# Inversion products of two batches packed on four tiles, and their copies made wide

## The reference

```python
# per batch, value head (32) and chunk (8 chunks of 64 tokens)
decay = jnp.where(tril, jnp.exp(g[..., :, None] - g[..., None, :]), 0.0)
M = jnp.where(stril, jnp.einsum('bhncd,bhnmd->bhncm', k_beta, k) * decay, 0.0)
T = jax.scipy.linalg.solve_triangular(eye + M, eye, lower=True)      # 64 x 64
v_c = T @ v_beta;  k_cumdecay = T @ (k_beta * exp(g))
# then a scan over the 8 chunks:
#   v_new = v_i - kcd_i @ state;  out = (q*exp(g)) @ state + (q k^T * dec) @ v_new
#   state = state * exp(g_last) + (k * exp(g_last - g))^T @ v_new
```

## Time and profile before

| | |
|---|---|
| median of 3 runs | 3193.22 us (3192.94 to 3195.3) |
| the profiled execution | 3193.03 us, span 3191.2 us |
| TensorE busy | 2911.1 us (91%) |
| VectorE busy | 1643.1 us (51%) |
| ScalarE busy | 1305.7 us (41%) |
| GpSimd busy | 1782.0 us (56%) |
| mean granted TensorE clock | 0.988 |

### The profile page before, as it was taken

One profiled execution on the slowest core, in us unless ns is written; L12 is line 12 of the kernel. 1 busy time (PEld: TensorE's weight loads), 2 busy tenths in 40 slices (PEclk: granted clock), 3 DMA queues, 4 the chain that ended last, 5 costly groups with the idle time before them and its releaser, 6 DMA issues.

```text
span 3191.2 us, 101541 instructions
## 1 busy us (share of the span) xinstructions
PE 2911.1 (91%) x41680; PEld 2122.0 (66%) x41680; DVE 1643.1 (51%) x2807; ACT 1305.7 (41%) x3046; POOL 1782.0 (56%) x1829
## 2 busy tenths in 40 slices
PE   2899999999999999999999999999999999999889
PEld 1566766766667666667766667677666667766744
DVE  4555555555555555655555555555545655555412
ACT  2443444444444444444444444444444444444311
POOL 1565555656655565665555566655555665555500
PEclk7899999999999999999999999999999999999999
DMA  2111110110111001011110101111011111110020
GB/s 83 27 30 29 30 22 19 27 35 24 30 29 27 20 22 34 24 30 29 30 29 9 35 24 30 30 29 31 13 29 27 29 29 29 30 25 9 3 61 20
DMA packets 71088, 89.52 MB, mean 28 GB/s; under 512 B 16720, under 2 KB 39376, under 8 KB 70608
## 3 DMA queue, kind: packets, MB, share of 16 engines
q1 hardware_dynamic: 70608, 82.74, 10.1%
HBM read 77.64 MB, written 5.08 MB: 26 GB/s over the span
## 4 chain that ended last, share of the span: by engine, by line
issue 35%; POOL 32%; PE 19%; DVE 7%; ACT 2%; POOLq 1%; DVEq 0%; DMA 0%; SPq 0%
POOL hT L1071 10%; POOL hT L1077 5%; PE ps L422 4%; POOL Kd L1094 4%; PE ps_state L537 3%; DVE St L931 3%; PE ps L510 3%; POOL Dm L1012 2%; POOL Sd L1035 2%; POOL Dm L1009 2%; PE ps L557 2%; POOL Kg L1094 2%; PE ps L611 2%; POOL A L1101 1%; PE ps_two L601 1%
## 5 line engine op out<-in xcount | busy, mean ns | idle before, releaser
L1035 POOL TENSOR_TENSOR Sd<-St,el 128x512 f32<-128x512 f32 x192 | 201.3, 1048 | 897.2 <-DVE St L928 843.4
L411 PEld LDWEIGHTS ps<-XW,U 64*64 64x64 f32 x10240 | 317.9, 135 | 125.8 <-issue 123.8
L411 PEld LDWEIGHTS ps<-XW,P 64*64 64x64 f32 x10240 | 311.8, 135 | 119.8 <-issue 119.8
L1071 POOL TENSOR_SCALAR hT<-idx_s,lutb 128x134 f32<-128x134 int32 x480 | 355.4, 744 | 27.5
L411 PE MATMUL ps<-XW,U 64*64 64x64 f32 x10240 | 342.9, 220 | 17.2 <-issue 12.7
L411 PE MATMUL ps<-XW,P 64*64 64x64 f32 x10240 | 333.6, 220 | 0.0
L834 DVE SCALAR_TENSOR_TENSOR cacc<-ps_two,cw,cacc 128x1022 f32<-128x1022 f32 (+2 forms) x192 | 245.7, 1280 | 97.1 <-ACT cacc L638 92.5
L923 DVE TENSOR_TENSOR Vn<-ps,bR 128x256 f32<-128x256 f32 x256 | 108.6, 424 | 350.3 <-PE ps L484 296.7
L834 DVE SCALAR_TENSOR_TENSOR cacc<-ps_state,cw,cacc 128x1022 f32<-128x1022 f32 (+2 forms) x192 | 245.7, 1280 | 78.5 <-ACT cacc L638 73.9
L382 PE MATMUL ps_two<-xnT,w_qkv 128*128 128x512 f32 x512 | 261.8, 636 | 20.4 <-DVEq L838 18.5
L711 ACT ACTIVATE P<-ps 128x512 f32<-128x512 f32 x320 | 184.2, 595 | 229.9 <-PE ps L411 229.3
(11 more groups left out here) (140 smaller groups left out, 5552.7 us busy)
## 6 DMA issues: line engine op xcount, KB each, us to landing
qg<-g_scratch SPq DMA_DIRECT2D x64, 512.0 KB, 7.4
g_st<-g_scratch SPq DMA_DIRECT2D x64, 256.0 KB, 5.7
w_qkv<-in_wqkvz SPq DMA_DIRECT2D x16, 512.0 KB, 3.8
w_z<-in_wqkvz SPq DMA_DIRECT2D x16, 256.0 KB, 3.1
w_o<-in_wout SPq DMA_DIRECT2D x16, 256.0 KB, 3.3
idx_s<-in_idx SPq DMA_DIRECT2D x32, 67.0 KB, 1.8
fw_scratch<-looked_up SPq DMA_DIRECT2D x32, 67.0 KB, 1.9
Kg<-in_x SPq DMA_DIRECT2D x2, 1024.0 KB, 7.6
```

The source lines that it names most:

```text
L411: m = pe.matmul(bank[r, c * C:(c + 1) * C], left[r, b, c, :], right[r, b, c, :], start=True, stop=True)
L1035: pool.tensor_tensor(Sd[:, :, :, :], St[:, c % 2, :, :, :], el[:, R.par, :, :, c].unsqueeze(3).broadcast_to([P, BB, RATIO, P]), ALU.mult). ...
L1071: m = pool.tensor_scalar(slots[k], idx_s[:, :], float(k), lutb[:, k:k + 1], ALU.is_equal, ALU.mult)
```

## The change

Both batches go through each step of the inverse together. `products` issues, for each chunk and head, one matmul of batch 0 on a diagonal tile and one of batch 1 on a tile off the diagonal, so that the four 64 x 64 tiles of the array are used in turn. A first product of batch 1 writes its result on the other half of the partitions; the second product therefore reads X of batch 1 from a copy with the halves exchanged, `Xs`, which ScalarE makes with two instructions per level (`swap`). The P1 copy, the masked copy and the turn become one instruction each for both batches, with masks twice as long in the constants. The banks 2 to 5 hold the two results (`ps_p1`, `ps_p2`); the four uses of `begin` go over four banks, no longer three; the last turn of the output moves from bank 5 to bank 1. VectorE issues the taps of kind lv - 2 at the end of level lv, one level later than before, and ScalarE its silu of a kind one level later too (the last one after the z gates).

```diff
-    small = [("z", i) for i in range(4)] + (N2 if nxt else []) + [("out", i) for i in range(4)]
+    small = [("z", i) for i in range(4)] + (N2 if nxt else [])
...
-        wide += [("p1", (lv, b)) for b in range(BB)] + [("p2", (lv, b)) for b in range(BB)]
+        levels += spread([("p1", (lv, b)) for b in range(BB)], (2, 3)) + spread([("p2", (lv, b)) for b in range(BB)], (4, 5))
...
-    return ahead + spread(small, (0, 1)) + spread(wide, (2, 3, 4)) + keys + spread(outs, (2, 3, 4)) + steps
+    return ahead + spread(small, (0, 1)) + spread(wide, (2, 3, 4, 5)) + levels + keys + spread(outs, (2, 3, 4)) + steps + ends
...
-HALF = NC * C // 2
+HALF = BB * NC * C // 2
...
-            def products(bank, b, left, right):
+            def products(banks, first):
+
                 pe.sem_inc(s["tiled"], 1)
                 for c in range(NC):
                     for a in range(RATIO):
-                        r = slice(a * C, (a + 1) * C)
-                        m = pe.matmul(bank[r, c * C:(c + 1) * C], left[r, b, c, :], right[r, b, c, :],
-                                      start=True, stop=True)
-                return m
+                        same, other = slice(a * C, (a + 1) * C), slice((1 - a) * C, (2 - a) * C)
+                        cols = slice(c * C, (c + 1) * C)
+                        if first:
+                            left = pe.matmul(banks[0][0][same, cols], U[same, 0, c, :], W[same, 0, c, :], start=True, stop=True)
+                            right = pe.matmul(banks[1][0][other, cols], U[same, 1, c, :], W[same, 1, c, :],
+                                              start=True, stop=True)
+                        else:
+                            left = pe.matmul(banks[0][0][same, cols], P1[same, 0, c, :], X[same, 0, c, :],
+                                             start=True, stop=True)
+                            right = pe.matmul(banks[1][0][same, cols], P1[other, 1, c, :], Xs[other, c, :],
+                                              start=True, stop=True)
+                left.then_inc(banks[0][1], 1)
+                right.then_inc(banks[1][1], 1)
...
                 for lv in range(1, LEVELS):
-                    for b in range(BB):
-
-                        pe.wait_ge(s["xs"], R.at(3 * (b + 1) if lv == 1 else 6 + (lv - 2) * 4 + 2 * (b + 1), 0, 24))
-                        bank, filled = wait_open(pe, R, "p1", (lv, b))
-                        products(bank, b, U, W).then_inc(filled, 1)
+                    pe.wait_ge(s["xs"], R.at(2 * lv, 0, 11))
+                    products([wait_open(pe, R, "p1", (lv, b)) for b in range(BB)], True)
                     beside(R, lv, 0)
...
+                    pe.wait_ge(s["x_c"], R.at(2 * lv, 0, 10))
+                    products([wait_open(pe, R, "p2", (lv, b)) for b in range(BB)], False)
                     beside(R, lv, 1)
...
+                    act.activation(P1[:, :, :, :].rearrange("p b c t -> p b (c t)"), ps_p1[:, :, :], ACT.Copy
+                                   ).then_inc(done[0], 1)
...
+                    if R.nxt and lv > 2:
+                        silu(R, lv - 3)
+                    if lv < LEVELS - 1:
+                        swap(R, lv)
                         if R.nxt:
-                            if lv > 1:
-                                silu(R, lv - 2)
                             tap0(R, lv - 1)
...
+            def swap(R, lv):
+
+                act.wait_ge(s["xs"], R.at(1 + 2 * lv, 0, 11))
+                for a in range(RATIO):
+                    act.activation(Xs[(1 - a) * C:(2 - a) * C], X[a * C:(a + 1) * C, 1], ACT.Copy).then_inc(s["x_c"], 1)
...
+                    dve.copy_predicated(odd(flat(X)), masks[lv - 1].rearrange("p (q n) -> p q n", n=n).bitcast(I32),
+                                        odd(flat(ps_p2))).then_inc(xs, 1)
+                    dve.wait_ge(xs, R.at(1 + 2 * lv, 0, 11))
                     for b in range(BB):
...
-                    if R.nxt and lv < 5:
-                        taps(R, lv - 1)
+                        dve.sem_inc(done[b], 1)
+                    if lv < LEVELS - 1:
+                        turn()
+                    if R.nxt and lv > 1:
+                        taps(R, lv - 2)
```

More of the change, by code:

```diff
@@ L192, in build @@
         ps_two = ctx.enter_context(nc.psum_tensor("ps_two", [P, BB, 512], F32))
-        ps = [ctx.enter_context(nc.psum_tensor(f"ps{i}", [P, 512], F32)) for i in range(2, 6)]
+        ps_p1 = ctx.enter_context(nc.psum_tensor("ps_p1", [P, BB, 512], F32))
+        ps_p2 = ctx.enter_context(nc.psum_tensor("ps_p2", [P, BB, 512], F32))
         ps_state = ctx.enter_context(nc.psum_tensor("ps_state", [P, RATIO, 512], F32))
-        ps = [ps_two[:, b, :] for b in range(BB)] + ps + [ps_state[:, a, :] for a in range(RATIO)]
+        ps = [t[:, n, :] for t in (ps_two, ps_p1, ps_p2, ps_state) for n in range(2)]
         both = {0: ps_two, 6: ps_state}
@@ L883, in begin @@
                 for b in range(BB):
-                    if b and last is not None:
-                        gated(last, 3)
                     dve.wait_ge(s["u_c"], R.at(2 * b + 2, 0, 4))
-                    dve.tensor_tensor(X[:, b], X[:, b], over_chunks(eye), ALU.add).then_inc(xs, 2)
-                    dve.wait_ge(xs, R.at(3 * b + 2, 0, 24))
-                    turn(b)
+                over_all = eye.unsqueeze(1).broadcast_to([P, BB * NC, C])
+                x_all = X[:, :].rearrange("p b c i -> p (b c) i")
@@ L891, in _, with turn @@
+                dve.tensor_tensor(x_all, x_all, over_all, ALU.add).then_inc(xs, 1)
+                if last is not None:
+                    gated(last, 3)
+                dve.wait_ge(xs, R.at(1, 0, 11))
+                turn()
             xs = s["xs"]
-            def turn(b):
-                dve.transpose(W[:, b].rearrange("p c i -> p (c i)"), X[:, b].rearrange("p c i -> p (c i)")
-                              ).then_inc(xs, 1)
+            def turn():
+                dve.transpose(flat(W), flat(X)).then_inc(xs, 1)
@@ L897, in invert @@
             def invert(R):
                 for lv in range(1, LEVELS):
-                    for b in range(BB):
[L901 to L910, removed]
-                        dve.wait_ge(xs, R.at(22 + b + 1 if lv == LEVELS - 1 else 6 + (lv - 1) * 4 + 2 * b + 1, 0, 24))
-                        dve.sem_inc(done, 1)
-                        if lv < LEVELS - 1:
-                            turn(b)
@@ L915, in invert, with odd @@
-                    if R.nxt and lv < 5:
-                        taps(R, lv - 1)
+                    done = [wait_full(dve, R, "p2", (lv, b))[1] for b in range(BB)]
+                    n = 1 << lv
+                    def odd(t):
+                        return t.rearrange("p (q d n) -> p q d n", d=2, n=n)[:, :, 1, :]
+                    dve.memset(carry[:, 1:2], 0.0)
+                    dve.copy_predicated(odd(flat(X)), masks[lv - 1].rearrange("p (q n) -> p q n", n=n).bitcast(I32),
+                                        odd(flat(ps_p2))).then_inc(xs, 1)
```

26 lines of the change are left out of this document (13 added, 13 removed).

## The result

The changed kernel takes 3405.04 us (median of 4 runs, 3404.6 to 3408.02) against 3194.26 us for the kernel before on the same chip (3192.94 to 3198.35): a ratio of 1.066, with an interval of 1.0641 to 1.0678. The profiled execution has a span of 3402.8 us. The forecast was 3414 us, slower, with a range of 3210 to 3485.

A forecast was written before the change was run, and what follows sets the result against it. TensorE was taken to bound the levels, with late taps stalling it after the change: 3193.0 + 20 (longer rounds) + 196 (clock falls) + 5 (last round, constants) = 3414 us; own range 3350 to 3480, 8-in-10 range 3210 to 3485.

The forecast's parts named there:

- The bound: Levels 1 to 5 of a round, 41.21 us, are bound by TensorE, with products and projections following without a gap.
- The products: On four tiles a product of both batches takes 1.08 us instead of 2.01; 1.75 us at 27 ns a record.
- Wide copies and turns: On VectorE, the wide masked copy takes 0.70 us (1.25 in level 1) and the wide turn 1.25 us.
- Rival 3: Faster: wide copy and turn cost no more than narrow ones, 0.43 and 0.71 us, giving 3107 us; chance 7%.
- Levels 3 to 5: Late taps on VectorE make TensorE wait before projections; turn to turn 9.2 us against 7.85, keys 1.0 us later.
- The ends: Outside the ordinary rounds: last round some 3 us longer, larger constants at the start 1 to 2 us.
- The clock: TensorE's 2.9 us idle waits, three a round, lower its clock: 2.3 falls a round at 2.75 us, 196 us.
- The signs: Listed evidence: products 1.1 us, copy 0.7, turn 1.25, waits 2.9, turn to turn 9.2 or more, clock 0.8 to 0.9.
- The sum: Whole kernel: 3193.0 + 20 for longer rounds + 196 for the clock + 5 for the ends = 3414 us.
- Rival 1: Clock kept or nearly despite TensorE's idle: 3218 us with no fall, 3303 with one per round; chance 22%.
- Rival 2: Four tiles bring little: products take 1.75 or 2.01 us, falls get fewer, 3360 to 3550 us; chance 13%.

The follow-up runs named there:

- filled kernel: Changed kernel plus three useless matmuls (512, 512 and 256 columns) behind the first products of levels 3 to 5, filling TensorE's wait: 3244.78 us, 1.0153.
- one matmul of 512 columns: Changed kernel plus one useless matmul of 512 columns behind the first products of levels 3 to 5: 3244.99 us, 1.0152.
- before, late taps: Kernel before the change with only the taps and ScalarE's silu moved one level later; two tiles and narrow copies stay: 3342.68 us, 1.0462.
- one matmul of 256 columns: Changed kernel plus one useless matmul of 256 columns behind the first products of levels 3 to 5: 3348.12 us, 1.0486.

## Why the prediction was right

**The bound.** Right. TensorE set the level before, and the change takes that away. The rest of the round is then set by whatever stands between a turn and the next masked copy. Two versions that differ in the place of the taps alone take 3405 and 3081 us.

**The products.** Right at the value taken, 1.08 us: 1.09 us were measured (1105.74 to 1106.83). The other end, 27 ns a record by the earlier trace rows, fell: 64 records in 1.09 us are at most 17 ns each. The Trainium skill, page "TensorE: Matmul & The Clock Gate", section "Wait — 56ns, not 53.3ns?", says that matmuls never start less than about 25 ns apart, however small. By it, as an estimate, the product would have taken 64 times 25 ns and 0.15 us for the start, 1.75 us. This trace does not agree: its 64 records take 1.09 us.

**Wide copies and turns.** Right: 0.71, 1.30 in level 1 and 1.25 us, for 0.70, 1.25 and 1.25. Rival 3 needed 0.43 and 0.71 and fell with that. The P1 copy (1.02 for 1.10) and the exchanges (1.28 for 1.1 a level) were near, and covered, as said.

**Levels 3 to 5.** The mechanism was right, down to the place of each wait: `proj` 4, `proj` 6 and the first z projection wait for L857. The idle time was 2.60 us instead of 2.9. In the filled kernel the round is 92.2 us against 91.2, +1.0 where the sum had +0.65. Two of its terms were short: from second product to copy it is 1.34 us and not 1.20 (1108.74 to 1110.08 in the changed kernel), and from copy to turn 0.24 and not 0.15.

**The ends.** The last round's term, 3 us, was mis-sized: from the second-to-last start of `keys_through` to the last one it takes 88.2 us in the filled kernel and 79.0 before, +9.2 us. Already by its own rows the term was small, since four or five levels of 0.99 us more each are 4 to 5 us. A level takes 7.80 us instead of the 5.76 worked out, since the clock is low there. This is one such level in the changed kernel, from copy to copy, and below it the last round's levels of the kernel before:

```profile
3180.10:3187.90 7.80, 3.97 (x128) 3.65 (x128) 1.94 (x5) 2.28 (x3) 7.25 (x9) 0.50 0.01 2
```

```profile
2970.00:2999.00 29.00, 26.16 (x643) 21.77 (x640) 10.49 (x29) 8.58 (x14) 17.54 (x24) 1.00 0.02 5
```

With no projections beside them, TensorE is idle for half of the time even so, and it stays at 1.2 GHz, where the same levels had 1.00 before. In the filled kernel the first `keys_through` starts 5.2 us later (167.3 for 162.1 us), and 2.4 us of this are there before the first projection starts. The larger constants show 1.3 us of that: their row has 1506.0 KB (not the 1521 of the prediction) and 11.0 us to landing, where it had 9.7; the rest was not traced. Four rounds are longer than the others in both kernels (95.3, 97.9, 95.3 and 98.4 us before, 99.3, 97.6, 99.2 and 99.2 filled). They grow by 8 us together, which the prediction did not look at. Two of the four hold a fall of the clock before and three in the filled kernel; no run explains the rest. In sum, for the filled kernel: 26 ordinary rounds 27, these four 8, the last 9, the start 5, and 2 behind the last `keys_through`: 51 us, where the prediction had 25.

**The clock.** Right in kind, that it falls behind these waits, and the total near: 160 us for 196. Two sizes were off, in opposite ways. There are 84 falls in 30 rounds, 2.8 a round (2.7 at the waits) where I took 2.3. And a fall costs 1.9 us where I took 2.75: from the first `keys_through` to the last the changed kernel takes 154 us more than the filled one, with 81 more falls. The windows above show two reasons. The clock is at 0.59 behind the first wait and already at 0.88 over the second product, so a fall need not cover a whole projection and the product behind it. And 44 of the 80 falls at the waits begin up to 1.3 us before the wait ends, when TensorE has no work to slow down.

**The signs.** One of those named was missed: a mean granted clock of 0.8 to 0.9. It was 0.929, below the 0.95 that would have spoken against the prediction.

**The sum.** 3194 + 51 + 160 = 3405 us, which is the measured time since both terms are differences to the filled kernel. The two errors, 26 us too little at full clock and 36 too much for the clock, nearly cancel; the forecast looks better than its terms were.

**The rivals.** Rival 1, the clock kept, gave 3218 us with no fall. The filled kernel is that case, at 3245 us. It did not come true: 80 of the 90 waits counted, of 2.60 us, have a fall. The Trainium skill, page "TensorE: Matmul & The Clock Gate", section "Why this matters for your kernels", warns only of gaps longer than these; this trace does not agree with that. Rival 2 fell with the products; the changed kernel with two tiles at a time is that case, at 3439 us with fewer falls, and lies in the 3360 to 3550 us that the rival gave. Rival 3, faster, fell with the wide operations. What neither forecast nor rivals said is how near the faster kernel was: with the taps a level earlier the same change gives 3.6%, with the first tap ahead of the exchange 5.3%.

## What to carry to other kernels

When the busiest engine gets shorter work, ask at once which queue sets the pace next, and what stands in that queue between two steps of the chain: here 3.9 us of taps that were free to run beside TensorE earlier, and cost 324 us where they stood. Count an idle gap of TensorE twice, once as time and once by what the clock takes from the work behind it; where a gap can't be removed, useless matmuls in it can pay (160 us here). Try to order work on the other engines anew after such a change, before judging it: the packing was worth 34 us with one order, after the falls of the clock that it brought, and 191 us with another.

## What the runs showed of the hardware

**The idle time in front of a fall of the clock.** Six kernels have a wait of their own size at the same place, 90 times from the first `keys_through` to the last round's levels. The table has the idle time before the projection in most of the 90, the falls in this stretch, and how many of them stand at such a wait:

| kernel | idle us | falls | at a wait |
|---|---|---|---|
| filled | 0.25 | 3 | 0 |
| one matmul of 512 columns | 1.54 | 4 | 0 |
| before, late taps | 1.62 | 1 | 0 |
| changed, two tiles | 1.85 | 32 | 27 |
| one matmul of 256 columns | 1.97 | 61 | 57 |
| changed | 2.60 | 84 | 80 |

The kernels differ in what TensorE does around the wait too, and the one with 256 columns has a fall behind a wait of 1.65 us, so this is no law of the gap alone. It shows how steep it is: 256 columns more of one useless matmul, 0.4 us of it, were worth 103 us (3348 against 3245).

**Four tiles.** Later fours of products come 0.058 us apart. In the kernel before the pairs of the same products come 0.058 us apart too, so four records take the time of two, as the prediction had it. The page "TensorEngine Tiling (Array Packing)" of the Trainium skill, section "PSUM Bottleneck", warns that packing can move the bound from TensorE to the copies out of PSUM. The run with the first tap ahead of the exchange agrees in part: VectorE fills most of its level of about 7.0 us, with 0.7 us for the masked copy out of PSUM and 3.9 us for the taps, which read the projection's two banks; the turn of 1.25 us reads no PSUM.

**Two batches, one after the other on two tiles each,** take 1.84 us for 64 records, not 2.01. The records start 29 ns apart on average, but between 0.76 and 0.93 us after the first, in the middle of the product, 13 of them start 15 ns apart. I read this as the second batch beginning while the last matmuls of the first still go, since the two use different tiles; the records do not name their batch.
